# Two spectral layers on one core: forward W transform folded over the two halves of a row, image layout folded with it, inverse W transform in 64x64 tiles

## The reference

```python
def layer0(x, w1, b1, w2, b2):
    f = fft2(x, axes=(H, W), norm="ortho")
    X = (f.real - f.imag)[:, rows, :23]              # 23 of 46 frequencies along W are kept
    o1 = relu(X @ w1[0] + b1[0])                     # 8 blocks of 48 channels
    o2 = o1 @ w2[0] + b2[0]
    return ifft2(softshrink(o2, 0.01)).real + x

def layer1(x, w1, b1, w2, b2):
    f = rfft2(x, axes=(H, W), norm="ortho")[:, rows, :23]
    o1r = relu(f.re @ w1[0] - f.im @ w1[1] + b1[0]);  o1i = relu(f.im @ w1[0] + f.re @ w1[1] + b1[1])
    o2r = shrink(o1r @ w2[0] - o1i @ w2[1] + b2[0]);  o2i = shrink(o1i @ w2[0] + o1r @ w2[1] + b2[1])
    return irfft2(o2r + 1j * o2i, norm="ortho") + x
```

## Time and profile before

| | us |
|---|---|
| median of the runs | 526.34 (525.83 to 531.92, 3 runs) |
| the profiled execution, own time | 527.67 |
| span of its profile | 525.8 |
| PE busy | 480.0 (91% of the span) |
| DVE busy | 303.9 (58%) |
| ACT busy | 208.8 (40%) |
| POOL busy | 172.8 (33%) |

### The profile page before, as it was taken

One profiled execution on the slowest core, in us unless ns is written; L12 is line 12 of the kernel. 1 busy time (PEld: TensorE's weight loads), 2 busy tenths in 40 slices (PEclk: granted clock), 3 DMA queues, 4 the chain that ended last, 5 costly groups with the idle time before them and its releaser, 6 DMA issues.

```text
span 525.8 us, 14875 instructions
## 1 busy us (share of the span) xinstructions
PE 480.0 (91%) x6144; PEld 347.5 (66%) x6144; DVE 303.9 (58%) x674; ACT 208.8 (40%) x473; POOL 172.8 (33%) x194
## 2 busy tenths in 40 slices
PE   4549999999999999999999999999999999998772
PEld 1137777767777677767777676777777777876531
DVE  6413456456764577456764577456763677566642
ACT  0014544554354433554354433454345433433101
POOL 9703133113432134313442133312442123222124
PEclk9858999999999999999999999999999999999967
DMA  8859955476899588877889688886989565735397
GB/s 187 268 141 218 272 149 150 105 205 181 253 222 244 154 210 246 238 202 184 263 216 236 173 208 242 228 213 176 255 221 248 167 175 156 156 84 141 108 242 223
DMA packets 76720, 104.65 MB, mean 199 GB/s; under 512 B 7761, under 2 KB 63303, under 8 KB 76526
## 3 DMA queue, kind: packets, MB, share of 16 engines
q1 hardware_dynamic: 57622, 55.97, 39.8%
q0 software_dynamic: 10608, 40.45, 29.1%
q10 hardware_dynamic: 8424, 7.28, 5.5%
HBM read 52.23 MB, written 51.43 MB: 197 GB/s over the span
## 4 chain that ended last, share of the span: by engine, by line
PE 79%; DMA 6%; DVE 6%; POOL 3%; ACT 2%; issue 2%; SPq 1%; ACTq 0%; POOLq 0%; DVEq 0%
PE ps L605 13%; PE ps L669 13%; PE ps L694 12%; PE ps L656 11%; PE ps L572 10%; PE ps L618 9%; PE ps L681 5%; PE ps L634 4%; DMA scr_f<-fs 3%; PE ps L644 3%; DVE img L551 2%; DVE ns L525 2%; ACT p L442 1%; POOL img L386 1%; POOL xs L369 1%
## 5 line engine op out<-in xcount | busy, mean ns | idle before, releaser
L551 DVE TENSOR_TENSOR img<-ps,img 90x768 f32<-90x768 f32 x92 | 82.7, 900 | 23.0 <-PE ps L605 18.1
L369 POOL TENSOR_TENSOR xs<-xs,nt 128x360 f32<-128x360 f32 (+1 forms) x48 | 41.5, 865 | 149.3 <-DVE nt L503 121.7
L605 PE MATMUL ps<-jr,cst 64*128 64x384 f32 (+1 forms) x358 | 83.6, 535 | 7.2 <-DVE img L551 5.7
L572 PE MATMUL ps<-img,cst 128*64 128x384 f32 (+1 forms) x368 | 72.2, 506 | 12.4 <-DMA img<-x 7.6
L378 POOL DMA_DIRECT2D y<-img x42 | 34.6, 825 | 136.0 <-DVE img L551 135.6
L618 PEld LDWEIGHTS ps<-cst,bt 128*64 128x64 f32 x1472 | 63.2, 141 | 21.0 <-issue 13.9
L435 ACT ACTIVATE o<-ps,wt 97x180 f32<-97x180 f32 (+1 forms) x96 | 33.8, 405 | 107.2 <-PE ps L656 107.1
L618 PE MATMUL ps<-cst,bt 128*64 128x90 f32 x1472 | 69.0, 248 | 6.7 <-DMA bt<-scr_f 6.7
L525 DVE SCALAR_TENSOR_TENSOR ns<-p,ps 109x384 f32<-109x384 f32 x96 | 53.2, 554 | 37.9 <-ACT p L442 33.0
L669 PE MATMUL ps<-wt,o 128*64 128x96 f32 x1472 | 73.9, 250 | 0.5 <-DVE o L517 0.5
L669 PEld LDWEIGHTS ps<-wt,o 128*64 128x64 f32 x1472 | 64.9, 137 | 12.6 <-issue 12.6
(11 more groups left out here) (41 smaller groups left out, 411.5 us busy)
## 6 DMA issues: line engine op xcount, KB each, us to landing
y<-img POOLq DMA_DIRECT2D x35, 540.0 KB, 5.5
img<-x POOLq DMA_DIRECT2D x30, 540.0 KB, 8.5
scr_i<-et SPq DMA_DIRECT2D x48, 270.0 KB, 5.7
scr_f<-fs SPq DMA_DIRECT2D x176, 72.0 KB, 3.4
bt<-scr_f SPq DMA_DIRECT2D x40, 270.0 KB, 4.6
jr<-scr_i SPq DMA_DIRECT2D x48, 216.0 KB, 5.1
img<-x ACTq DMA_DIRECT2D x10, 540.0 KB, 7.4
y<-img SPq DMA_DIRECT2D x11, 270.0 KB, 3.8
```

The source lines that it names most:

```text
L369: nc.gpsimd.tensor_tensor(re, re, nt[s % 2][:, :, 0:kws(s), 0:H], ALU.subtract).then_inc(re_ok, 1)
L551: nc.vector.tensor_tensor(y, p, y, ALU.add).then_inc(i_add, 1)
L572: last = mm(ps[64 * r:64 * r + 64, P3 + g % 2, 0:(b - a) * HC], K["w_fwd"], img[t % IMGS][:, a:b, :].rearrange("p h c -> p (h c)"), start= ...
L605: last = mm(ps[:, B0 + r, 0:n], K["w_inv"][64 * r:64 * r + 64, :], set_rows(t, j)[64 * r:64 * r + 64, at, 0:n], start=True, stop=True)
```

## The change

- The image buffers are laid out folded: `img[k]` is [128, 23, 2, 192]. Image row h = 23p + j lies on partitions 64p to 64p+44 (p = 0, 1), and the second free axis r tells which half of the row (columns 0 to 44, or 45 to 89). All 128 partitions are cleared once, for images 1 and 2 after the forward groups of task 0 (`clear`).
- A new piece of work, `uv`: DVE adds and POOL subtracts the two halves of 8 image rows (4 j and both p), 128x768 elements each, into `uv[2]`. The even frequencies are computed from the sum, the odd ones from the difference.
- `fwd` works on 8 rows in 8 matmuls of tile shape 64x32, 384 streamed columns each: 6 groups a task in place of 12. ACT copies each group by two instructions of 128x384, in task 0 too. SP stores each group by 8 DMAs of 36 KB (before 2 of 72 KB for half as many rows). `fs` has 3 buffers of twice the size.
- `inv` works on one half r of the columns of 8 rows, in 4 matmuls of tile shape 64x64; 12 groups a task as before. In the list they stand before c0, between d1 and d0, and after t; one step in six has four, and the fourth stands before e. Their counts in steps 3, 4, 5, 0 are 2, 3, 4, 3. The rows of `scr_i` come in 6 sets of 2 DMAs (147 KB each), through 4 buffers `jr`.
- Image loads and stores come in 4 chunks of 16, 16, 8 and 5 rows, two DMAs each (one for each p), not in 6 chunks of 8 rows with one DMA. `refill` of chunk 0 stands in step 5 of a task, of chunk 1 in step 0 of the next, of chunks 2 and 3 in its step 1.
- The scratch tensors are padded from 45 to 48 rows and ordered anew; `e` computes 96 columns, not 90.

The core of the diff:

```diff
+WR, HR = W // 2, -(-H // 2)
+CH = -(-HR // 4)
+ROWS = 64 + WR
+GROUPS = 2 * CH
+CHUNKS = [(0, 2), (2, 4), (4, 5), (5, 6)]
+IMGS, FS, BT, JR = 3, 3, 3, 4
+LAST_POOL = (1, 4, 7, 9)
...
-            fwd[s] = [("fwd", t + 1, 4 * (i - 1) + k) for k in range(4)]
+            fwd[s] = [("fwd", t + 1, 2 * (i - 1) + k) for k in range(2)]
         if i >= 3 and 0 < t < TASKS - 1:
-            inv[s] = [("inv", t - 1, 3 * (i - 3) + k) for k in range(3)]
+            inv[s] = [("inv", t - 1, g) for g in ((0, 1), (2, 3, 4), (5, 6, 7, 8))[i - 3]]
...
+        first, last = inv[s][0:len(inv[s]) - 3] if len(inv[s]) > 3 else [], inv[s][max(len(inv[s]) - 3, 0):]
+        uv = [("uv",) + f[1:] for f in fwd[s]]
+        ahead = [("uv",) + f[1:] for f in fwd[s + 1]] if s + 1 < NSTEPS else []
...
-        order += inv[s][0:1]
+        order += first
         if s > 1:
             order.append(("e", s - 2))
-        order += inv[s][1:2]
+        order += uv[1:2]
+        order += last[0:1]
         if s < NSTEPS:
             order.append(("c0", s))
         if 0 < s <= NSTEPS:
             order.append(("d1", s - 1))
+        order += last[1:2]
         if s < NSTEPS:
             order.append(("d0", s))
+        if i == 5 and t > 0:
+            order.append(("refill", t - 1, 0))
+        if i == 0 and t > 1:
+            order.append(("refill", t - 2, 1))
...
-        order += fwd[s][0:2]
+        order += fwd[s][0:1]
         if s + 1 < NSTEPS:
             order.append(("a", s + 1))
         if i == 1 and 0 < t < TASKS:
             order += [("rows", t - 1, j) for j in range(JR)]
+        if i == 1 and t > 1:
+            order.append(("refill", t - 2, 2))
+        order += fwd[s][1:2]
...
+        order += last[2:3]
+        order += ahead[0:1]
+        if i == 1 and t > 1:
+            order.append(("refill", t - 2, 3))
...
 SP:
-                    sp.wait_ge(f_cp, n + 1)
-                    for r in range(f_dmas(g)):
-                        a, b = h0 + 2 * r, min(h0 + 2 * r + 2, h1)
-                        sp.dma_start(scr_f[t][a:b].rearrange("h e k c -> (e k) h c"),
-                                     fs[k][64 * r:64 * r + 2 * KWP, 0:(b - a) * HC].rearrange("q (h c) -> q h c", c=HC)).then_inc(f_st[k], 16)
+                    for p in range(2):
+                        sp.wait_ge(f_cp, 2 * n + p + 1)
+                        for a in range(2):
+                            for o in range(2):
+                                sp.dma_start(scr_f[t][o * KWP // 2:(o + 1) * KWP // 2, :, p, g, a].rearrange("k e s c -> (k e) (s c)"),
+                                             fs[k][64 * a + 32 * o:64 * a + 32 * o + KWP, p, :]).then_inc(f_st[k], 16)
...
 POOL:
+                if kind == "uv":
+                    t, g = what
+                    n, (j0, j1) = t * CH + g, jrange(g, g + 1)
+                    pool.wait_ge(*x_loaded(t, g))
+                    if n >= 2:
+                        pool.wait_ge(f_mm, n - 1)
+                    nc.gpsimd.tensor_tensor(uv[n % 2][:, 1, 0:j1 - j0, :], img[t % IMGS][:, j0:j1, 0, :], img[t % IMGS][:, j0:j1, 1, :],
+                                            ALU.subtract).then_inc(v_ok, 1)
+                if kind == "refill" and what[0] + IMGS < TASKS:
+                    t, c = what
+                    k, (b, f) = t % IMGS, divmod(t + IMGS, HALVES)
+                    pool.wait_ge(y_st[k][c], 32 * (t // IMGS + 1))
+                    for p in range(2):
+                        j0, j1 = jrange(*CHUNKS[c], p)
+                        pool.dma_start(folded(k, p, j0, j1), rows_of(x[b], HR * p + j0, HR * p + j1, f)).then_inc(x_ld[k][c], 16)
...
 ACT:
+                    for p in range(2):
+                        nc.scalar.activation(fs[n % FS][:, p, :], ps[:, P3 + p, 0:2 * HC], ACT.Copy).then_inc(f_cp, 1)
...
 DVE:
+                if kind == "uv":
+                    ...
+                    nc.vector.tensor_tensor(uv[n % 2][:, 0, 0:j1 - j0, :], img[t % IMGS][:, j0:j1, 0, :], img[t % IMGS][:, j0:j1, 1, :],
+                                            ALU.add).then_inc(u_ok, 1)
...
 PE, fwd:
-                    for r in range(f_dmas(g)):
-                        a, b = h0 + 2 * r, min(h0 + 2 * r + 2, h1)
-                        last = mm(ps[64 * r:64 * r + 64, P3 + g % 2, 0:(b - a) * HC], K["w_fwd"],
-                                  img[t % IMGS][:, a:b, :].rearrange("p h c -> p (h c)"), start=True, stop=True)
+                    pe.wait_ge(u_ok, n + 1)
+                    pe.wait_ge(v_ok, n + 1)
+                    vacate(0)
+                    vacate(1)
+                    for a in range(2):
+                        for o in range(2):
+                            for p in range(2):
+                                q, m = 64 * p, 64 * a + 32 * o
+                                last = mm(ps[m:m + 32, P3 + p, 0:2 * HC], w_fwd[q:q + 64, o, :],
+                                          uv[n % 2][q:q + 64, o, 2 * a:2 * a + 2, :].rearrange("w s c -> w (s c)"), start=True, stop=True)
...
 PE, inv:
-                    for r in range((h1 - h0 + 1) // 2):
-                        n = min(2, h1 - h0 - 2 * r) * HC
-                        last = mm(ps[:, B0 + r, 0:n], K["w_inv"][64 * r:64 * r + 64, :], set_rows(t, j)[64 * r:64 * r + 64, at, 0:n], start=True, stop=True)
+                    for p in range(2):
+                        for a in range(2):
+                            m, c = (min(2, HR - 4 * g - 2 * a)) * HC, slice(64 * a, 64 * a + 64)
+                            last = mm(ps[64 * p:64 * p + 64, B0 + a, 0:m], w_inv[c, r, :], set_rows(t, g)[c, p, 0:m], start=True, stop=True)
```

328 lines of the change are left out of this document (163 added, 165 removed).

## The result

| | before | after |
|---|---|---|
| median of the runs, us | 526.92 (525.83 to 531.92, 4 runs) | 591.17 (586.58 to 601.0, 4 runs) |
| ratio | | 1.117, 95% interval 1.1035 to 1.1304 |
| profiled execution, own time, us | 527.67 | 594.54 |
| span, us | 525.8 | 592.6 |
| mean granted clock of TensorE | 0.969 | 0.947 |

The ratio compares the means of the runs within 1.5% of each kernel's fastest, which leaves out the 601.0; by the two medians it would be 1.122.

A forecast was written before the change was run, and what follows sets the result against it. PE's work was taken to set the time in the middle. The terms -20.5 + 5.2 + 4.5 + 8 + 3 + 6 = +6.2 on the profiled 527.7 gave 533.9, as a median 533 us; range 513 to 556.

The forecast's parts named there:

- the price on PE: Forward groups on PE: 0.72 us plus 0.1 for shape change, -20.5 us in all; inverse groups +5.2 us.
- the rival of +32 us: Forward groups on PE: four column tiles don't run side by side, groups last two more passes; 565 us, chance 0.06.
- the start: Before the first `a`: 48 SP store issues of 0.48 us back to back, +8 us, between -1 and +10.3.
- the wait in step 3: PE's forward group waits 0.75 us for DVE's add of the inverse group between d1 and d0; +4.5 us.
- The end: Last inverse group of task 6 whole, +1, and larger final stores, +2; together +3 us (0 to 5).
- POOL, SP and the DMA engines in steps 1 and 2: Full POOL, SP's queue and DMA bytes over capacity: 1.2 us a task in five tasks, +6 us (0 to 27).
- a rival of chance 0.26: Late refills: chunk 1's and those behind it land late, holding up c1's ReLU and d1; 547 us, chance 0.26.
- 1.5 to 3 steps until its use: Image refills: the time each had before the change, against a landing of 8.5 us (4.2 to 10.2).
- DVE and POOL hinder each other in uv: POOL's `uv` piece waits DVE's out, 2.77 us in place of 1.82; +13 us, 546, chance 0.05.
- a subtraction above 2.5 us: Sign of port contention: POOL's `uv` subtraction lasting longer than that.
- hidden behind PE: DVE's 48 `uv` adds of 0.95 us, 46 us in all, cost nothing; DVE goes from 37 to about 45 us a minute.
- just about covers it: SP's queue in step 1: loads come 4 to 8 us later, but are issued two steps ahead.

The follow-up runs named there:

- e7: e5 without `uv`: sum and difference left out, forward matmuls read the image directly; 560.8 us, ratio 1.0627.
- e13: e11 without `uv` (sum and difference left out); 535.1 us, ratio 1.0174.
- e5: The changed kernel with six image chunks of one group each and every refill issued earlier; 574.6 us, ratio 1.0906.
- e3: The changed kernel with both halves of `uv` on DVE, none on POOL; 602.1 us, ratio 1.1441.
- e9: e8 with both halves of `uv` on DVE; 557.4 us, ratio 1.0589.
- e8: The changed kernel with e5's refills, e4's stores and the inverse groups back before e, after e and after t; 571.7 us, ratio 1.0842.
- e11: e9 with three inverse groups in each of steps 3, 4, 5, 0, no fourth; 554.1 us, ratio 1.0539.
- e10: e7 with e4's stores; 536.7 us, ratio 1.0192.
- e4: The changed kernel with 4 larger scratch-store DMAs at each forward group in place of 8; 595.7 us.

## Why the prediction was wrong, point by point

**Right: the price on PE.** A forward group holds PE 0.80 us with its change of shape (257.59 to 258.39), predicted 0.72 + 0.1; four tiles do run side by side over the array's columns, so the rival of +32 us falls. Where nothing is late the gain is 1.0 us a step (e7 and e13, interval 2, which holds two forward groups); predicted were 2.9 us a task, 0.97 a step. An inverse group holds PE 0.70 us ahead of a stage of the same shape (277.53 to 278.23). The 0.86 us a task predicted for the inverse groups was not measured by itself: the middle tasks of e13, the one with the stall apart, are 0.6 to 2.0 us shorter than before, where -2.9 + 0.86 = -2.0 was predicted, for other places of these groups. The rule of the Trainium skill ("TensorEngine Tiling (Array Packing)", section "Tiling Modes") agrees again: in the changed kernel the same inverse group holds PE 0.70 us ahead of c0, which has its shape, and 0.80 ahead of e (554.38 to 555.18), which has another.

**Right: the start,** +8.9 us for +8, the first `a` at 40.1 (38 to 41 was named), behind 48 issues in 21.5 us. They came mostly 0.41 us apart, not 0.48, and with one gap of 1.8 us. **Right in kind and size: the wait in step 3,** 5.9 us in six waits of PE's forward group for DVE's add, for 4.5; at 269.57 it is 1.04 us. Not predicted was a further wait of the inverse group itself (0.78 us at 267.36). **Not come:** POOL near 60% of the span; it was 47%. **The end** was mis-sized: +7.1 for +3; 5 us of it is PE's wait for the row loads of the last task, which I had not looked at. I had priced the stores.

**Wrong, the first and largest: "POOL, SP and the DMA engines in steps 1 and 2", +6 us.** This is the step that failed, by its size. The mechanism was there, as a rival of chance 0.26, and its signature (PE idle before d1, released by DVE, which itself waited for the image load) is what the profile shows. The size was wrong: 27 us in step 1, 3.6 to 6.5 a task, where I took 1.2; e5 took 18 of it away. Within it, what was wrong is "1.5 to 3 steps until its use", which I granted to every refill but chunk 1's. It was chunk 0's that came late. Its two halves were issued from 228.4 on, and DVE wanted them from 238.5 on, 10 us later; the second landed after 14.3 us where the earlier trace rows had at most 10.2. The DMA engines were full in all of that time, which lies in step 0 and the first half of step 1, while my byte count looked at steps 1 and 2. I had computed an overload there and then taken each landing time from a kernel without it.

**Wrong: "DVE and POOL hinder each other in uv", chance 0.05.** The contention is real and changes both: DVE's piece takes 0.95 us alone (e3, e9), 1.90 in the mean and up to 4.1 beside POOL (e5). Its net price is 14 us (e8 to e9), predicted 13 if it came; that the two agree is luck, since the path is another. I had rated it by the fact that no row of before showed it; the earlier trace rows only held adds with one input in PSUM, so they said nothing about it either way. The Trainium skill's rule ("GPSIMD Engine Reference", section "Key points") was right, and it deserved the weight that silence of the trace leaves, not 0.05. The picture of POOL waiting DVE out was half of it. It does so where DVE begins first, and the sign that I had named, a subtraction above 2.5 us, is there in 18 of 40 pieces of the changed kernel. What costs PE time is the other half, which I had not thought of: DVE waits POOL out just as well, and longer, since POOL's pieces are twice as long (e5: 1904 ns in the mean, with POOL's at 2066), and behind DVE's piece stands a ReLU.

**Wrong: "hidden behind PE" for the work of `uv` itself.** With both pieces on DVE, e11 and e13 differ by 19 us, on one chip. DVE is busy 45 to 46 of 60 us in the middle of e11, so the average has room; but `uv` stands in front of a ReLU that PE needs 1 us later. I had priced the cover by DVE's busy share and not by what stands behind each piece in its order.

**Wrong: SP's queue "just about covers it".** 16 stores in a step, three steps in a row, push the last one so far back that `bt` of the next task comes late; e7 to e10 prices it, with the stores' landing and the clock behind it, at 24 us once the rest is gone. In the changed kernel itself it shows no more than in e4, nothing that can be told, since the refills make PE late first.

**Left out: the clock.** No term held that waits make work slower. 63 us at the lower level against 33 is worth up to 15 us, the 44 against none of the middle up to 22, and it belongs to each wait above: from 60 to 480 us e9 and e10 have 3 us at the lower level and e11 none.

**How the 64 us divide.** By medians, each with its share of the clock, in the order in which I took the losses away: refills 17 (e5), stores and inverse places 3 (e8; no difference by their intervals), contention 14 (e9), the fourth inverse group 3 (e11; its interval meets e9's), the work of `uv` 19 (e13), what remains 9. Another order would share it otherwise, as e3 and e4 show: each edit alone gave nothing or less. Of "what remains", start and end are shown, and the stall in e13's step 3 is open; which of the row loads' waits at the end could be avoided was not tried.

**The shape of the error.** Every term but PE's lay on the same side, and I added them at their likely values to a sum of +6 with a range up to +30. They are not independent: all of them stand in steps 1 and 2, on engines whose order is fixed, where the second begins when the first is paid. At the bounds that I had written down (refills 27, contention 13, start 10.3, end 5, the wait 6, inverse 6.5, forward -20.5) the sum is +47 against the profiled +67; SP's queue, the work of `uv` and the clock, which had no bound, are the rest.

## What to carry to other kernels

When work moves from a saturated engine to idle ones, don't price it by their busy shares: list, for every moved instruction, what stands behind it in that engine's order and how soon the bound engine wants that. A refill's landing time measured in one kernel (4.2 to 10.2 us here) need not hold in a stretch that is full in the other (up to 14.6); a load that was never late needs its slack recomputed too, not only the one made larger. And a first experiment that removes a true cause can show nothing (e3, e4), because another wait covers it: remove causes in combination before discarding one.
